# A softmax bound that runs on over two halves, in an attention and soft-MoE layer on one core

## What is computed

```python
q = apply_rope(q); k = apply_rope(k)                       # 16 heads of 16
logits = jnp.einsum('bhid,bhjd->bhij', q, k) * SCALE
logits = jnp.einsum('bhij,gh->bgij', logits, Wpre)
attn = jax.nn.softmax(logits, axis=-1)
attn = jnp.einsum('bhij,gh->bgij', attn, Wpost)
out = jnp.einsum('bhij,bhjd->bhid', attn, v)
...
x = _layernorm(x + attention, axis=-1)
x = _layernorm(x + moe(x), axis=-1)
```

## Time and profile before

| | us |
|---|---|
| median of 3 runs | 8534.67 (8532.32 to 8536.32) |
| the profiled execution | 8543.35 |
| its span, first to last instruction | 8541.5 |

### The profile page before, as it was taken

One profiled execution on the slowest core, in us unless ns is written; L12 is line 12 of the kernel. 1 busy time (PEld: TensorE's weight loads), 2 busy tenths in 40 slices (PEclk: granted clock), 3 DMA queues, 4 the chain that ended last, 5 costly groups with the idle time before them and its releaser, 6 DMA issues.

```text
span 8541.5 us, 453588 instructions
## 1 busy us (share of the span) xinstructions
PE 8043.4 (94%) x182764; PEld 4656.4 (55%) x182764; DVE 7627.7 (89%) x13390; ACT 6951.9 (81%) x11648; POOL 6613.4 (77%) x14053
## 2 busy tenths in 40 slices
PE   7999999998899999999889999999978999999997
PEld 4555555555455555555545555555554555555554
DVE  7999999996899999999689999999968999999996
ACT  5888888886688888888568888888856888888884
POOL 6788888884778888888478888888847888888883
PEclk9999999998999999999899999999989999999998
DMA  1010111112101111111211111111121011111112
GB/s 52 23 27 25 27 25 27 25 26 89 33 24 26 27 25 25 27 26 26 88 34 25 26 26 25 27 26 26 25 87 35 24 25 27 25 27 26 26 25 90
DMA packets 265786, 284.31 MB, mean 33 GB/s; under 512 B 41089, under 2 KB 252673, under 8 KB 261377
## 3 DMA queue, kind: packets, MB, share of 16 engines
q1 hardware_dynamic: 263680, 255.07, 11.1%
HBM read 78.75 MB, written 39.85 MB: 14 GB/s over the span
## 4 chain that ended last, share of the span: by engine, by line
PE 57%; issue 15%; DVE 13%; POOL 10%; ACT 2%; POOLq 1%; DVEq 1%; DMA 0%; SPq 0%; ACTq 0%
PE psS L1257 34%; PE psP L1276 12%; PE psO L1291 6%; DVE big L890 4%; DVE spare L879 3%; POOL pl L561 2%; DVE pl L918 2%; ACT big L706 2%; POOL rh L601 2%; PE psM L1302 1%; POOL rl L606 1%; POOL nm L569 1%; POOL at L489 1%; DVE ot L901 1%; PE psS L1387 1%
## 5 line engine op out<-in xcount | busy, mean ns | idle before, releaser
L1257 PE MATMUL psS<-KH,AX 64*128 64x512 f16 x32768 | 3893.4, 377 | 77.2 <-DMA AX<-AX 50.1
L890 DVE SCALAR_TENSOR_TENSOR big<-psP,big 128x512 f16<-128x512 f32 x4096 | 2626.2, 682 | 323.3 <-ACT big L706 322.5
L706 ACT ACTIVATE big<-psP 128x512 f16<-128x512 f32 x4096 | 2205.3, 590 | 785.0 <-PE psP L1276 752.4
L879 DVE CUSTOM_DVE_ANT_0 spare<-psS,lift 128x1024 f16<-128x1024 f32 x2048 | 2487.9, 1215 | 188.6 <-PE psS L1257 187.4
L687 ACT ACTIVATE pr<-psS,nb 128x1024 f32<-128x1024 f32 x2048 | 2286.9, 1117 | 146.6 <-DVE nb L879 140.9
L1257 PEld LDWEIGHTS psS<-KH,AX 64*128 64x128 f16 x32768 | 1475.9, 94 | 1575.6 <-issue 75.3
L716 ACT ACTIVATE ph<-pr 128x1024 f16<-128x1024 f32 x2048 | 2165.4, 1057 | 64.7
L1257 PE MATMUL psS<-KL,AX 64*128 64x512 f16 x16384 | 2110.6, 376 | 0.0
L918 DVE TENSOR_TENSOR pl<-pr,ph 128x1024 f16<-128x1024 f32 (+1 forms) x2048 | 2086.3, 1019 | 0.0
L1276 PEld LDWEIGHTS psP<-rh,ph 64*128 64x128 f16 x32768 | 1462.6, 95 | 732.8 <-DVE big L890 550.4
L1276 PE MATMUL psP<-rh,ph 64*128 64x64 f16 x32768 | 1681.7, 191 | 188.7 <-DVE big L890 154.9
(11 more groups left out here) (137 smaller groups left out, 6470.3 us busy)
## 6 DMA issues: line engine op xcount, KB each, us to landing
AX<-AX SPq DMA_DIRECT2D x2048, 64.0 KB, 2.0
ph<-in_xT SPq DMA_DIRECT2D x16, 512.0 KB, 9.3
xr<-in_x SPq DMA_DIRECT2D x64, 128.0 KB, 2.3
Q<-in_w SPq DMA_DIRECT2D x8, 1024.0 KB, 7.2
out<-V SPq DMA_DIRECT2D x16, 512.0 KB, 3.9
d_x<-x SPq DMA_DIRECT2D x60, 128.0 KB, 2.1
d_xn<-xn SPq DMA_DIRECT2D x60, 128.0 KB, 2.0
d_lg<-lg SPq DMA_DIRECT2D x60, 128.0 KB, 2.0
```

What stands on the lines that cost most here:

```text
L706: a.activation(PT[:, hf * JH:(hf + 1) * JH, :, 0, i0:i0 + HQ], psP[:, ih, :].rearrange("p (j g i) -> p j g i", j=JH, g=H), ACT.Copy, scale ...
L879: v.tensor_tensor_reduce(out=spare[:, :], in0=psS[:, 2 * h:2 * h + 2, :].rearrange("p c n -> p (c n)"), in1=lift[:, 0:1].broadcast_to([P, ...
L890: v.scalar_tensor_tensor(out=PT[:, js, :, 1, i0:i0 + HQ], in0=psP[:, ih, :].rearrange("p (j g i) -> p j g i", j=JH, g=H), scalar=MDROP, in ...
L1257: mm = pe.matmul(psS[:, 2 * hp + half, :], AX[rows, k8, kq, s_, :], K_[rows, kq, hp, :], start=n == 0, stop=n == len(steps) - 1, tile_posi ...
```

## The change

Four edits, which belong together:

- half_max of half 1 starts its running minimum from nb of half 0 instead of from the constant. nb of half 1 is then the bound over the whole row, and the second exponential needs no factor.
- lower_bound and nm are gone. factor makes one column, exp(nb1 - nb0), the factor of half 0. The other column of ff is set to 1.0 once, ahead of everything.
- total is one instruction: sums0 x ff0 + sums1, a tensor_scalar with two per-partition operands. ws is gone.
- Two places in the order change. On GpSimd total stands ahead of mixq. On ScalarE factor stands ahead of highs of half 1.

```diff
@@ gpsimd
+            g.memset(ff[:, :, :], 1.0).then_inc(s_carry, 1)
...
-                def lower_bound(T, t):
-
-                    p = t % 2
-                    g.wait_ge(s_nb, T * 2 + 2 + 1)
-                    apart(g)
-                    g.tensor_scalar(nm[:, p:p + 1], nb[:, p, 0:1], nb[:, p, 1:2], None, ALU.min).then_inc(s_nm, 1)
-
                 def total(T, t):
 
                     p = t % 2
                     g.wait_ge(s_exp, T * 2 + 2 + 1)
                     g.wait_ge(s_f, T + 1 + 1)
-                    g.tensor_tensor(ws[:, p, :], sums[:, p, :], ff[:, p, :], ALU.mult).then_inc(s_ws, 1)
-                    g.wait_ge(s_ws, T + 1 + 1)
-                    g.tensor_tensor(tot[:, p:p + 1], ws[:, p, 0:1], ws[:, p, 1:2], ALU.add).then_inc(s_tot, 1)
+                    apart(g)
+                    g.tensor_scalar(tot[:, p:p + 1], sums[:, p, 0:1], ff[:, p, 0:1], sums[:, p, 1:2],
+                                    ALU.mult, ALU.add).then_inc(s_tot, 1)
...
                     if one:
-                        lower_bound(T - 1, t_1)
+                        total(T - 1, t_1)
                     if live:
                         mixq(it, t + LEAD, first and t + LEAD < TG)
-                    if one:
-                        total(T - 1, t_1)
                     roots(it, t, 0)
@@ scalar
-                    a.wait_ge(s_nm, T + 1 + 1)
+                    a.wait_ge(s_nb, T * 2 + 2 + 1)
                     if not early:
                         a.wait_ge(s_r0, T - 2 + 1 + 1)
-                    a.activation(ff[:, p, :], nb[:, p, :], ACT.Exp, bias=nm[:, p:p + 1], scale=-1.0).then_inc(s_f, 1)
+                    a.activation(ff[:, p, 0:1], nb[:, p, 0:1], ACT.Exp, bias=nb[:, p, 1:2], scale=-1.0).then_inc(s_f, 1)
...
                         exps(T, t, 1, early)
+                        factor(T, t, early)
                         highs(T, t, 1, early)
-                        factor(T, t, early)
@@ vector
-                                           in1=lift[:, 0:1].broadcast_to([P, N2]), scale=-SSCALE, scalar=-LOW,
+                                           in1=lift[:, 0:1].broadcast_to([P, N2]), scale=-SSCALE, scalar=nb[:, t % 2, 0:1] if h else -LOW,
```

More of the change, by code:

```diff
@@ L139, in seq_layer @@
         sums = sb("sums", [P, 2, 2])
-        nm = sb("nm", [P, 2])
         ff = sb("ff", [P, 2, 2])
-        ws = sb("ws", [P, 2, 2])
         rc = sb("rc", [P, 2])
@@ L246, in seq_layer @@
         s_nb = sem("s_nb")
-        s_nm = sem("s_nm")
-        s_ws = sem("s_ws")
         s_f = sem("s_f")
@@ L289, in seq_layer @@
         s_out = sem("s_out")
-        FROM_ONE = [s_A, s_nb, s_nm, s_ws, s_f, s_tot, s_rec, s_r0, s_rp, s_rh, s_rl, s_pl, s_plg, s_D, s_F, s_y, s_exp, s_ph,
+        FROM_ONE = [s_A, s_nb, s_f, s_tot, s_rec, s_r0, s_rp, s_rh, s_rl, s_pl, s_plg, s_D, s_F, s_y, s_exp, s_ph,
                     s_mh, s_ml, s_oc, s_CTc, s_t1, s_xb, s_st, s_nw, s_out, s_er]
```

## The result

The changed kernel takes 8400.76 us (median of 4 runs, 8394.93 to 8404.49), the kernel before in the same comparison 8533.49 us. The ratio is 0.9849 with a 95% interval of 0.9836 to 0.9861: 133 us or 1.5% faster. The profiled execution's span fell from 8541.5 to 8400.9 us.

The account below looks back on a forecast made before the run. Bound: VectorE's rc waiting for GpSimd's late tot in plain and Newton slots. Gains 0.72 + 1.14 less 0.24 net 1.62 us per iteration; 58 x 1.62 + 7 = 101 us, forecast 8434 us, range 8385 to 8515 (own 8405 to 8465).

Parts of the forecast that it names:

- Which wait ends last: VectorE ahead of rc: it waits for GpSimd's late tot, 0.20 us to give in plain slots, 0.43 in Newton slots.
- The plain and Newton slots: Slots 0, 1, 8, 9 (plain) give 0.72 us per iteration; slots 13 to 15, after Newton root steps, give 1.14.
- the floor of 6.60: Slot length after the change: VectorE's floor rises from 6.53 to 6.59, TensorE's is 6.58, so slots end at about 6.60.
- the loss in slots 3, 7, 11 and 12: Second pass on VectorE: the per-partition operand costs 0.06 us where VectorE bounds the slot, 0.24 us per iteration.
- The slots taken as TensorE's: Slots 2, 10 (output matmuls) and 4 to 6 (small matmuls): TensorE bounds them and they stay unchanged.
- The other iterations: Each batch's first iteration has some 10 plain slots, 7 us in all; the irregular last ones are counted half.
- The order of total on GpSimd: tot, placed ahead of at, ends 0.3 us after the hold instead of 1.18; rc's wait goes in all slots.
- the race: After VectorE's pl, GpSimd's work up to tot (1.18 us) against VectorE's pass up to rc (1.14 us).
- GpSimd as the bound: Rival: GpSimd's loop sets the slots if tot is too long; slower, 8650 us at x = 0.9; chance 0.09.
- The rival's loop: GpSimd's plain-slot loop, 6.09 us plus tot's time x; back at today's slot times at x = 0.65.
- The pass that holds GpSimd: Rival: VectorE's second pass with lift and nb blocks GpSimd for about 1.15 us; 9165 us, chance 0.03.
- The gain given back at VectorE's pl: Rival: rr slips 0.1 us behind rc, so each VectorE pl waits 0.1 for GpSimd's pl; 8505 us, chance 0.10.

## Why the prediction was right

**Which wait ends last** was read correctly. rc's lateness was on the path in plain and Newton slots, and it is gone in every slot (1.14 to 1.15 us behind the pass). The prediction put the time at 8434, the runs at 8401, inside the range and 0.4% below the forecast. Of its signs most came: plain slots 0, 8 and 9 at 6.57 to 6.59, the second pass at 1.279, tot at 0.34. Newton slots came at 6.55 to 6.61, a little below the 6.6 to 6.7. TensorE's wait ahead of its first psP shrank but did not go: in the plain slot its weight load waited 0.23 us, 0.51 before.

**The plain and Newton slots** were slightly under-sized. The sum gave them 0.72 and 1.14 us per iteration, they gave 0.85 and 1.31. One of the four plain slots was misread: slot 1 lasted 7.30 us, not 6.78, because VectorE's long pl collides there with xb, and it is the slot of the earlier trace rows. It gave 0.26 all the same. The term at fault is the floor of 6.60: the step that raised VectorE's floor from 6.53 to 6.59 by the operand's 0.06 had overlooked that the 6.53 contains some 0.05 of pl waiting for GpSimd's pl (it took 1.26 in that slot), and that a later pl does not wait. What remained in slots 0, 8 and 9 is 6.57 to 6.59, in which TensorE has no idle time. The run with the constant rules VectorE out as their bound; ScalarE, with 0.03 us idle, was not tested. Slots 12 and 13 came in at 6.55, so 6.58 is no strict floor. The price of the operand itself was right (0.06 forecast, 0.063 measured), and so was the loss in slots 3, 7, 11 and 12 (0.24 against 0.22). That this sum fits is partly luck: the four changed by +0.10, +0.05, +0.09 and -0.03. Taking the operand away again gave 0.06 in each of the first three and 0.02 in the last; the rest of slots 3 and 11 goes with their collision, where the short pl rose from 1.13 and 1.09 to 1.17.

**The slots taken as TensorE's** were not quite still: slot 6 gave 0.17 and slot 4 0.05 that the sum did not have, and slot 5 lost 0.04. Which wait ended there stays open.

**The other iterations** gave 9.9 + 6.5 us, where the sum had 7 and about 3.

**The order of total on GpSimd** was the step whose reason failed while its result held. The prediction wanted tot first so that it wins the race, and said of the new wait that it "costs nothing". In the runs the race alone would have been nearly won behind mixq too. What total's place brings is that GpSimd is waiting, with nothing in execution, at the moment VectorE's pl starts. The wait is worth 0.6% by itself (0.9938 against 0.9875), the order the remaining 0.3%.

**GpSimd as the bound** was drawn too near. The rival's loop was 6.09 + x, with the decision at x = 0.65. With x doubled to 0.64 plain slots did not move. In the changed kernel the loop is 4.00 us from rr (1172.00) to the end of pl (1176.00), 1.50 to the end of tot (one slot earlier, from 1169.42 to 1170.92), and 0.80 on to rr with nothing else to wait for, as the run with two totals shows (1178.41 to 1179.21). That is 6.30, and 6.60 with the second total, an estimate that just reaches the 6.58 that the slots last anyway; the formula had 6.73 for it. Its mistake was to add the hold and tot's own time in full, 1.27 + 0.34, where the two take 1.50 together, and to read 4.06 for the 4.00. At x = 0.65 the formula gives a plain slot 6.74, so only the Newton slots would have been back at their old time there. x itself was 0.34, at the upper end of 0.19 to 0.35.

**The pass that holds GpSimd** did not occur. The second pass with lift and nb from SBUF runs beside AX and rl, which keep their 0.67 and 0.42 us. What the page "SBUF — State Buffer" of the Trainium skill left open is answered for this form: beside lift and with the scores in PSUM, a per-partition operand does not count as a second SBUF input.

**The gain given back at VectorE's pl** was given 0.10. It did not happen in the changed kernel. With nm kept it did, and as described: rr slips behind rc, and GpSimd's pl is in front of VectorE's, which takes 1.40. With total behind mixq and with both orders old VectorE's pl is late by the same rule, but it is at that stands in front of it.

## What to carry to other kernels

Where VectorE and GpSimd share work, look at what GpSimd is executing in the 0.1 us before each VectorE instruction with two SBUF inputs. A semaphore wait placed there was worth 0.6% here, more than total's saved step (0.1%), and a reordering by one place cost 0.9%. A short instruction is priced by the chain it stands in, here 1.8% for 0.27 us and the wait on it. An edit without a net effect may be two effects that cancel, so read it by kind of slot and not by its total.

## What was not expected of the hardware

- A one-column tensor_scalar on GpSimd takes 0.19 us with immediates, 0.27 with one per-partition operand, 0.34 with two.
- When VectorE's pl and a GpSimd instruction meet, less than 0.1 us decides which of them is held: VectorE's pl 0.07 us behind at took 1.41 us instead of 1.21; 0.02 us behind AX it took 1.20 instead of 0.68; 0.06 us ahead of rh it took 0.68 and rh 0.78 instead of 0.29.
- A per-partition start value costs VectorE's pass 63 ns (1279 against 1216) and does not hold GpSimd, whose AX and rl beside it keep their 0.67 and 0.42 us.
